# A graph network layer pair on one core: x1 scattered to edge slots and to a second part of its table instead of stored whole

## What is computed

```
h   = relu(layernorm(x))
agg = segment_sum(relu(h[src] + edge_attr), dst)
z   = relu(batchnorm((h + agg) @ W1 + b1)) @ W2 + b2      # norms over all nodes
x1  = x + h + relu(graphnorm(graph_layernorm(z)))         # a scale and a shift per channel
h1  = relu(layernorm(x1))
out = x1 + relu(h1 @ W + segment_sum((h1 @ M)[src], dst))
```

## Time and profile before

| | |
|---|---|
| median of three runs | 2896.22 us (2890.07 to 2901.19) |
| the profiled execution's own time | 2903.93 us |
| its span, first to last instruction | 2902.1 us |
| mean granted TensorE clock | 0.926 of full speed |
| moved by DMA | 531.88 MB, mean 183 GB/s |
| stage 1, 2, 3, 4 (read from the timeline) | 0 to 595, 595 to 1780, 1785 to 2525, 2530 to 2902 us |

### The profile page before, as it was taken

One profiled execution on the slowest core, in us unless ns is written; L12 is line 12 of the kernel. 1 busy time (PEld: TensorE's weight loads), 2 busy tenths in 40 slices (PEclk: granted clock), 3 DMA queues, 4 the chain that ended last, 5 costly groups with the idle time before them and its releaser, 6 DMA issues. The chain is left out here.

```text
span 2902.1 us, 50615 instructions
## 1 busy us (share of the span) xinstructions
PE 2524.3 (87%) x12305; PEld 2126.5 (73%) x12305; DVE 2085.8 (72%) x5779; ACT 1724.4 (59%) x3492; POOL 1730.7 (60%) x1633
## 2 busy tenths in 40 slices
PE   6778878789999999999999997787887888878887
PEld 5667667568888888888888885676676777757766
DVE  6677777658888888888888986455555555456665
ACT  4777677646666666666666664566565666534443
POOL 4555555557777777767777762555554555436564
PEclk8889899889999999999999999889888888989999
DMA  8888777531444444444444444788888886444442
GB/s 203 190 191 204 200 196 210 138 103 56 140 161 150 155 150 150 153 160 156 155 150 150 154 152 182 270 299 304 294 285 286 304 297 226 153 123 127 133 133 87
DMA packets 276275, 531.88 MB, mean 183 GB/s; under 512 B 70860, under 2 KB 158659, under 8 KB 276150
## 3 DMA queue, kind: packets, MB, share of 16 engines
q1 hardware_dynamic: 215846, 459.78, 48.0%
q0 software_dynamic: 59712, 70.24, 9.3%
q10 hardware_dynamic: 592, 0.54, 0.1%
HBM read 340.43 MB, written 287.04 MB: 216 GB/s over the span
## 5 line engine op out<-in xcount | busy, mean ns | idle before, releaser
L1513 POOL DMA_INDIRECT x1d_table<-x1r,slot x391 | 381.5, 976 | 348.1 <-issue 178.5
L1066 POOL DMA_INDIRECT ar<-sum_table,idx x391 | 480.1, 1228 | 177.5 <-issue 95.0
L1113 ACT ACTIVATE r<-pair,bnC,bnA 128x512 f32<-128x512 f32 (+1 forms) x396 | 307.5, 777 | 381.8 <-PE pair L1314 356.1
L1739 PE MATMUL pair<-Ws,h1T 128*128 128x256 f32 x1564 | 423.1, 432 | 105.3 <-DVE orr L1647 97.6
L1221 DVE CAST rH<-r 128x512 fp32r<-128x512 f32 (+1 forms) x396 | 395.5, 999 | 95.2 <-ACT r L1113 83.1
L1739 PEld LDWEIGHTS pair<-Ws,h1T 128*128 128x128 f32 x1564 | 336.7, 221 | 167.4 <-issue 103.9
L881 PE MATMUL bank<-hr 128*128 128x257 f32 (+1 forms) x1564 | 318.5, 361 | 50.9 <-ACT hr L593 26.0
L881 PEld LDWEIGHTS bank<-hr 128*128 128x128 f32 x1564 | 283.6, 214 | 91.3 <-issue 29.4
L1647 DVE SCALAR_TENSOR_TENSOR orr<-pair,x1r 128x1024 f32<-128x1024 f32 (+1 forms) x99 | 119.9, 1211 | 313.6 <-DMA sum_table<-e_tot 164.4
L1330 PE MATMUL bank<-rH,W2h 128*128 128x512 f32 (+1 forms) x792 | 307.5, 388 | 2.2 <-ACT yr L1127 2.2
L1330 PE MATMUL bank<-rL,W2h 128*128 128x512 f32 (+1 forms) x792 | 307.3, 388 | 0.0
(11 more groups left out here) (240 smaller groups left out, 5398.9 us busy)
## 6 DMA issues: line engine op xcount, KB each, us to landing
xr<-in_x SPq DMA_DIRECT2D x130, 384.0 KB
x_table<-x1r SPq DMA_DIRECT2D x97, 512.0 KB
out<-orr SPq DMA_DIRECT2D x97, 512.0 KB
xr<-in_x SPq DMA_DIRECT2D x89, 512.0 KB
xh_table<-xr SPq DMA_DIRECT2D x89, 512.0 KB
yT_table<-yr SPq DMA_DIRECT2D x89, 512.0 KB
xh_kept<-xh_table SPq DMA_DIRECT2D x57, 512.0 KB
y_stays<-yT_table SPq DMA_DIRECT2D x57, 512.0 KB
```

The lines of the kernel that those rows point to most:

```text
L1066: pool.indirect_dma_start(ar[0:p, s, j, :], None, sum_table[:, :], bass.IndirectOffsetOnAxis(ap=idx[0:p, s, j:j + 1], axis=0), bounds_chec ...
L1113: act.activation(r32[:, m, 0:n], z_ps[m][:, 0:n], ACT.Relu, bias=bnC[:, m:m + 1], scale=bnA[:, m:m + 1]).then_inc(r_kept, 1)
L1513: pool.indirect_dma_start(x1d_table[:, :], bass.IndirectOffsetOnAxis(ap=slot[0:p, part, s * TW + j:s * TW + j + 1], axis=0), x1r[0:p, s, j ...
L1739: last = pe.matmul(tile_of(pair[2], j)[0:p, :], h1T[:, s, c, j * P:j * P + p], Ws[:, c, :], start=c == 0, stop=c == KC - 1)
```

## The change

- x1 is no longer stored whole. `x1_table` has two parts: 12,672 edge slots as before, and behind them one row per node (`FREE` rows in all). Stage 3's scatter sends a target's row to its slot, the row of another source to its row in the second part, and skips the rest. The store of x1 (line 1464), its semaphores and the waits on them go. Stage 4 and the early gathers read source rows at a looked-up place, `index[:, :, 1]`.
- The places are made in stage 2 on POOL, between its gathers and additions: 99 scatters write slot numbers of sources into `source_table` (one after the other), it is read back at group 49, joined with `ids` on DVE between two rounds (`join_places`, before group 52), stored as `place_table` at group 54, and 99 look-ups read the place of each edge's source at groups 55 to 95. The store of `index_table` moves from stage 1's SP to POOL at group 97. POOL's groups are all written out instead of a loop.
- `sum_table` gets 128 rows of zeros, and `id_table` starts with their numbers. The gather of stage 2 reads a row for every node, so the memset of `ar`, the copy of the indices and the wait go.
- SP clears the first part of `x1_table` from the zero rows (DRAM to DRAM) and, with one more DMA per group, 500 rows of the second part, as five copies of 100 zero rows.
- At the head of stage 2 the order of PE, ACT and DVE changes (below); five products with zeros at the end of stage 1 go (the last real product closes each accumulation); `sb` aligns all tiles to 64 bytes.

```diff
+FREE = ET * P + NODES
+CLEAR, CLEARS = 100, 5
+MIDDLE = 13
...
-    sum_table = nc.dram_tensor("sum_table", (ET * P, CH), FP32, kind="Internal").ap()
+    sum_table = nc.dram_tensor("sum_table", (ET * P + P, CH), FP32, kind="Internal").ap()
...
-    x1_table = nc.dram_tensor("x1_table", (NODES, CH), FP32, kind="Internal").ap()
-    x1d_table = nc.dram_tensor("x1d_table", (ET * P, CH), FP32, kind="Internal").ap()
+    x1_table = nc.dram_tensor("x1_table", (FREE, CH), FP32, kind="Internal").ap()
+    source_table = nc.dram_tensor("source_table", (NODES, 1), I32, kind="Internal").ap()
+    place_table = nc.dram_tensor("place_table", (NODES, 1), I32, kind="Internal").ap()
...
-    size = 4 * math.prod(shape[1:])
-    return scope.enter_context(nc.sbuf_tensor(name, shape, dt, side=side, align_bytes=512 if size >= 512 else 64))
+    return scope.enter_context(nc.sbuf_tensor(name, shape, dt, side=side, align_bytes=64))
...
+        sp.wait_ge(blank_ids, 1)
         sp.dma_start(id_table[0:P * TILES, :].rearrange("(p t) a -> p (t a)", t=TILES),
                      no_rows[:]).then_inc(ids_clear, 16)
         sp.dma_start(id_table[P * TILES:NODES, :], no_rows[0:REST, 0:1]).then_inc(ids_clear, 16)
+        sp.wait_ge(consts, 1)
+        sp.dma_start(source_table[0:P * TILES, :].rearrange("(p t) a -> p (t a)", t=TILES),
+                     no_source[:]).then_inc(blank_out, 16)
+        sp.dma_start(source_table[P * TILES:NODES, :], no_source[0:REST, 0:1]).then_inc(blank_out, 16)
+        sp.dma_start(sum_table[ET * P:ET * P + P, :], zeros[:, 0:CH]).then_inc(blank_out, 16)
...
-        sp.dma_start(index_table[:, :, :], index[:]).then_inc(index_out, 16)
...
+        pool.iota(no_rows[:], [[0, TILES]], base=ET * P, channel_multiplier=1).then_inc(blank_ids, 1)
...
+        dve.tensor_scalar(source_slot[:], src_f[:], float(ET * P), None, ALU.add)
...
-                if is_int(at[0]) and at[0] == 0:
-                    sp.wait_ge(blank_made, 1)
-                sp.dma_start(x1d_table[bass.ds(at[0] * P, P), :], blank[:]).then_inc(slots_clear, 16)
-
+                sp.dma_start(x1_table[bass.ds(at[0] * P, P), :], sum_table[ET * P:ET * P + P, :]).then_inc(slots_clear, 16)
+                clear(at[0])
+        def clear(i):
+            first = i * CLEAR * CLEARS + ET * P
+            sp.dma_start(x1_table[bass.ds(first, CLEAR * CLEARS), :].rearrange("(a p) c -> a p c", a=CLEARS),
+                         sum_table[ET * P:ET * P + CLEAR, :].rearrange("(a p) c -> a p c", a=1).broadcast_to(
+                             [CLEARS, CLEAR, CH])).then_inc(slots_clear, 16)
+        for i in range(ET, NODES // (CLEAR * CLEARS)):
+            clear(i)
         rounds(sp, step, WHOLE - 2, NU, NPEEL, NW - WHOLE + 2 + 6)
-        sp.wait_ge(slots_clear, 16 * ET)
...
+        def gather(k):
+            s = k % AU
+            p, n = wide_shape(k)
+            after(pool, t2_made, k - AU + 1)
+            pool.nop(nofuse=True)
+            for j in range(n):
+                c = k * TW + j
+                pool.indirect_dma_start(ar[0:p, s, j, :], None, sum_table[:, :],
+                                        bass.IndirectOffsetOnAxis(ap=ids[0:p, c:c + 1], axis=0),
+                                        bounds_check=ET * P + P - 1, oob_is_err=False
+                                        ).then_inc(a2_in[s], 16)
+        def residual(k):
+            s, h = k % NU, k % AU
+            p, n = wide_shape(k)
+            pool.wait_ge(h2n_done, k + 1)
+            pool.nop(nofuse=True)
+            pool.tensor_tensor(xbuf(k, s)[0:p, 0:n, :], xbuf(k, s)[0:p, 0:n, :], hr[0:p, h, 0:n, :],
+                               ALU.add).then_inc(xh2_done, 1)
+        def place_source(t):
+            after(pool, sources_out, 16 * t)
+            pool.nop(nofuse=True)
+            pool.indirect_dma_start(source_table[:, :],
+                                    bass.IndirectOffsetOnAxis(ap=index[:, t, 0:1], axis=0),
+                                    source_slot[:, t:t + 1], None, bounds_check=NODES - 1,
+                                    oob_is_err=False).then_inc(sources_out, 16)
+        def load_places():
+            pool.wait_ge(sources_out, 16 * ET)
+            pool.wait_ge(places_set, 1)
+            pool.nop(nofuse=True)
+            pool.dma_start(places[:, 0:TILES], source_table[0:P * TILES, :].rearrange(
+                "(p t) a -> p (t a)", t=TILES)).then_inc(places_in, 16)
+            pool.dma_start(places[0:REST, (NW - 1) * TW:(NW - 1) * TW + 1],
+                           source_table[P * TILES:NODES, :]).then_inc(places_in, 16)
+        def store_places():
+            pool.wait_ge(places_joined, 3)
+            pool.nop(nofuse=True)
+            pool.dma_start(place_table[0:P * TILES, :].rearrange("(p t) a -> p (t a)", t=TILES),
+                           places[:, 0:TILES]).then_inc(places_out, 16)
+            pool.dma_start(place_table[P * TILES:NODES, :],
+                           places[0:REST, (NW - 1) * TW:(NW - 1) * TW + 1]).then_inc(places_out, 16)
+        def look_up(t):
+            if t == 0:
+                pool.wait_ge(places_out, 32)
+                pool.nop(nofuse=True)
+            pool.indirect_dma_start(index[:, t, 1:2], None, place_table[:, :],
+                                    bass.IndirectOffsetOnAxis(ap=index[:, t, 0:1], axis=0),
+                                    bounds_check=NODES - 1, oob_is_err=False).then_inc(looked_up, 16)
+        def sources(k, half):
+            if 2 <= k < 48:
+                first = (2 * (k - 2) + half) * ET // 92
+                for t in range(first, (2 * (k - 2) + half + 1) * ET // 92):
+                    place_source(t)
+            if k == 49 and half == 0:
+                load_places()
+            if k == 54 and half == 1:
+                store_places()
+            if 55 <= k < 96:
+                first = (2 * (k - 55) + half) * ET // 82
+                for t in range(first, (2 * (k - 55) + half + 1) * ET // 82):
+                    look_up(t)
+            if k == 97 and half == 0:
+                pool.wait_ge(looked_up, 16 * ET)
+                pool.nop(nofuse=True)
+                pool.dma_start(index_table[:, :, :], index[:]).then_inc(index_out, 16)
+        for k in range(NW + 2):
+            if k < NW:
+                gather(k)
+            if k == 1:
+                pool.memset(places[:], NO_ROW).then_inc(places_set, 1)
+            sources(k, 0)
+            if k >= 2:
+                residual(k - 2)
+            sources(k, 1)
+        pool.wait_ge(index_out, 16)
...
+        def join_places():
+            dve.wait_ge(places_in, 32)
+            dve.tensor_scalar(targets[:], ids[:], float(ET * P), float(FREE), ALU.is_ge,
+                              ALU.mult).then_inc(places_joined, 1)
+            dve.wait_ge(places_joined, 1)
+            dve.tensor_tensor(targets[:], targets[:], ids[:], ALU.add).then_inc(places_joined, 1)
+            dve.wait_ge(places_joined, 2)
+            dve.tensor_tensor(places[:], places[:], targets[:], ALU.min).then_inc(places_joined, 1)
...
+        add((0, 0, 0, NU))
         dve.wait_ge(q_made, 1)
-        link(dve.tensor_copy(small[:, 0:2, :], pair[1][:, 0, 0:8].rearrange("p (a b) -> p a b", a=2)))
...
+        keep_low((0, 0, 0, NU))
...
-        add((0, 0, 0, NU))
         add((1, 1, 0, NU))
-        keep_low((0, 0, 0, NU))
-        rounds(dve, step, WHOLE - 2, NU, NPEEL, NW - WHOLE + 2 + 2)
+        rounds(dve, step, WHOLE - 2, NU, NPEEL, NW - WHOLE + 2 + 2, join_places)
...
-            turn(back(at, -1))
+            first = is_int(at[0]) and at[0] == 0
+            if not first:
+                turn(back(at, -1))
             for m in range(HC):
                 hidden(at, m)
+                if first and m == 1:
+                    turn(back(at, -1))
                 output(back(at, 1), m)
...
+        for m in range(HC):
+            for l in range(KC):
+                pe.matmul(bank[0][:, 4 + m:5 + m], W1s[:, l, m * P:m * P + P], mh[:, l:l + 1],
+                          start=l == 0, stop=l == KC - 1)
...
-            two = back(at, 2)
-            if inside(two, NW):
-                k = two[0]
-                s, _ = ring(two, RU)
-                p, n = wide_shape(k)
-                sp.wait_ge(x1_done, k + 1)
-                sp.dma_start(wide_rows(x1_table, k), x1r[0:p, s, 0:n, :]).then_inc(x1_out[s], 16)
...
-            pool.tensor_copy(slot[:, part, :], ids[:, bass.ds(first * TW, RU * TW)]
+            pool.tensor_copy(slot[:, part, :], places[:, bass.ds(first * TW, RU * TW)]
...
-                pool.indirect_dma_start(x1d_table[:, :],
+                pool.indirect_dma_start(x1_table[:, :],
                                         bass.IndirectOffsetOnAxis(ap=slot[0:p, part, s * TW + j:s * TW + j + 1], axis=0),
-                                        x1r[0:p, s, j, :], None, bounds_check=ET * P - 1,
+                                        x1r[0:p, s, j, :], None, bounds_check=FREE - 1,
```

(12 more changed lines are left out.)

95 lines of the change are left out of this document (36 added, 59 removed).

## The result

The changed kernel takes 2975.97 us (median of 4 runs, 2956.43 to 2981.68), the kernel before beside it 2898.60 (2890.07 to 2901.19, 4 runs): a ratio of 1.0258, interval 1.0229 to 1.0287. It is 2.6% slower; the forecast was 4.4% faster, and the range ended at 2890. The profiled execution took 2981.68 us, span 2980.0, beside 2903.9 and 2902.1 before.

What follows compares the result with a forecast made beforehand. It took stage 3 as bound by DMA and stage 2 by PE. Stage 3 -145, stage 2 +20, its head -9 and stage 1 +6 sum to -128 us, giving 2768 us on the median's scale; range 2700 to 2890.

Steps and rivals of the forecast that it cites:

- Stage 3 is bound by DMA: Stage 3 before the change: 2.20 MB per group at 298 GB/s is 7.4 us, matching the group's 7.5 us.
- the term of -145 us: Stage 3: without x1's stores a group falls from 7.45 to 5.95 us over 97 groups; bounds -205 and -92.
- Rival D: Stage 3 hardly moves: costly scattered rows or another wait hold the group at 7 us; total 2865, chance 0.06.
- sign of being wrong altogether: Stage 3 over 7 us per group, or stage 2 over 1310 us.
- 356 GB/s if the queues filled completely: Stage 3: at this rate a group's 1.77 MB would take 5.0 us, under PE's 5.2 us.
- Stage 2, +20 (0 to +60): Stage 2: added DMA hides under PE's 11.87 us, POOL is at the edge; 0.2 us charged on 99 groups.
- Rival C: Stage 2: waits of place scatters and look-ups make POOL's period 12.6 us, +70 us; total about 2820, chance 0.13.
- A: Stage 2: the clear runs on five of 16 engines, 4.5 us instead of 1.4, losing 20 to 80 us; chance 0.22.
- B: Stage 2: five engines and 1 KB pieces, 7.1 us per clear, +310 us; whole near 3070, chance 0.10.
- Alignment: Tiles at multiples of 64 bytes: stage 1's leave 256-byte boundaries, the big tiles of stages 2 and 3 stay aligned.
- Head of stage 2, -9 (-4 to -12): Start of stage 2: reordered work brings the first hidden product earlier; 1 us from five zero products dropped in stage 1.
- Stage 1, +6: Stage 1: extra clears ahead of the loads and tiles off 256-byte boundaries cost 6 us, bounds 0 and +20.

Runs made afterwards that it cites:

- a_noload: Changed kernel with only the first twelve groups' xh and yT loaded in stage 3; ratio to the kernel before 1.0237.
- a_oob: Changed kernel with all four scatters of a group issued in stage 3 but every index out of range, so no row is sent; ratio to the kernel before 1.0282.
- a_three: Changed kernel with stage 3 scattering three of a group's four tiles; ratio to the kernel before 0.9617.
- b_gather: Kernel before without stage 3's scatters into x1d_table, stage 4 gathering target rows from x1_table; ratio to the kernel before 0.9743, on another occasion 1.0433.
- a_all: Changed kernel with a POOL pause in stage 3, clears of 16 x 32 rows and larger tiles aligned to 256 bytes; 2578.9 us, ratio to the kernel before 1.0289.
- a_again: Changed kernel run once more, unaltered, on another chip; 2575.37 us against 2508.38 for the kernel before, ratio 1.027.

## Why the prediction was wrong

- **"Stage 3 is bound by DMA"**, the step that failed, and with it the term of -145 us, of which 1.3 came. Its evidence was `orr`'s idle time behind a DMA, read as the `out` store, and 2.20 MB per 7.4 us, which fits any cause of 7.4 us. What held the group were TensorE's late signals behind POOL's runs of eight scatters. a_noload (DMA 0.26, same group) shows it isn't DMA, a_oob and a_three that it is POOL's issuing. Rival D had the time of the group, by another mechanism, at 0.06; it named POOL's 5.1 us, for which I had argued only that it lies under PE's. The prediction's own sign of being wrong altogether, stage 3 over 7 us per group, came: 7.21.
- **"356 GB/s if the queues filled completely"**: b_gather moved 361 GB/s over 400 us of stage 3 at 0.92, at 5.3 us per group, with x1's stores. So the stores fit under TensorE's pace; the stores and the scatters together at that pace no run shows (5.4 us by the estimate above).
- **Stage 2, +20 (0 to +60)**: it cost 84, of which the experiments place 50 and 21 and leave some 9 (a_all's 1140.5 us against 1131.8). Rival C's mechanism was right for the index scatters, 50 us of waits, not for the look-ups. What I missed is why a landing takes so long; I let the addition of 2.41 us cover it, and it took up to 5.7 us more.
- **Rivals A and B**: A's price was right: the two packets of each of five engines take 4.4 us, where I had 4.5, and B's pieces of 1 KB at 7.1 us did not come (they are of 50 KB). I priced the clear as load on engines and found it just over the period. Its shape cost 50 us, not through the clear's own time but through that wait. A and C were one chain, and I gave them 0.22 and 0.13 as alternatives, each with stage 3's gain in it.
- **Alignment**: I called stage 2's big tiles still aligned and charged only stage 1. Stage 2 lost 20 us to it.
- **Head of stage 2, -9 (-4 to -12)**: from TensorE's first instruction of the stage to the first hidden product 22.4 us became 18.8, so -3.6. **Stage 1, +6**: the first addition stood 5.3 us earlier instead of 3 (both terms together); the same stage 1 ended between 595.3 and 617.4 in other runs of the changed kernel, so nothing can be said of it. **Stage 4, 0**: 0.5.

Range and sign failed together, because all rivals but D kept stage 3's gain, B too, the only slower one, whose price lay in stage 2 alone.

## What to carry to other kernels

Bytes over time equal to a plausible rate don't make DMA the bound: ask whether the stage follows when the bytes go (here a run without the loads would have told it before any table was redesigned), and check the releaser that a profile names against the landing it stands for. A DMA share near 1 isn't the bound either: in stage 3 of b_gather (1900 to 2300 us) and of a_again (1800 to 2200) it is 0.92 and 0.96 while TensorE is busy 98% of the time and sets the pace. An indirect DMA that waits for the landing of the one before it inherits the whole queue's delay; let it wait for one several back, and give every large copy beside it a leading dimension of 16, not of 5. Compare kernels on more than one occasion, and watch the kernel before each time: b_gather is 2.6% ahead where that takes 2880 us and 4.3% behind where it takes 2506.

## What the hardware showed beyond that

- In stage 3 TensorE's semaphore signals came 4.3 to 4.9 us late, all together 1.1 to 1.8 us behind the end of POOL's run, when a product ended 6 to 8 us into an unbroken run of eight indirect DMAs, also when these moved no byte. Six microseconds aren't a threshold: in stage 1 of the kernel before, in POOL's runs of 6.5 to 9 us, none of 17 signals was late in the first microsecond, and all 16 that fell 3 to 4 us into a run were, by 5.0 us in the median. The longest delay there is 8.4 us. 120 of the signals of stage 1 and 215 of stages 3 and 4 in the kernel before came over 0.3 us late, and none in the three traces of the better condition; the kernel before is 374 us faster there. The Trainium skill ("SBUF — State Buffer", SBUF: two separate sides) has TensorE never wait for another engine's port; that is about ports, and no run here shows which path the signals wait on.
- It isn't TensorE's signals alone: in stage 1 some 150 of VectorE's came over 0.3 us late too, by up to 5.5 us, and none of ScalarE's (kernel before and changed kernel).
- A product 128x512 took 395 ns with tiles at multiples of 64 bytes and 390 at multiples of 256 (stage 2's output layer).
- A clear of 512 KB from DRAM to DRAM as 5 x 100 rows cost the kernel 50 us more than as 16 x 32 rows, with a mean DMA share of 0.61 and 0.67 (700 to 1150 us): the mean over the engines hid that only five at a time worked on it, at some 23 GB/s each.
